# Reordering the gating front end of a convolution-and-attention kernel: a quarter of the moments on ScalarE, set-up products moved, parameter loads on another queue

## What is computed

```python
# L0: group norm, then a mixture of 4 experts, two of them for each pixel
g = gn(x)                                     # 32 groups of 3 channels, moments over 3*784 values
scores = softmax(tokens(g) @ gate_w + gate_b) # one row for each of 32*784 tokens, 4 experts
top_v, top_i = top_k(scores, 2); top_w = softmax(top_v)
present = one_hot(top_i).any(over tokens)     # which expert is first, which second anywhere
y_e = w2_e @ relu(w1_e @ g + b1_e) + b2_e     # 96 -> 96 -> 96 channels
coef_e = sum_k present[k, e] * top_w_k        # k = 0, 1
x = x + sum_e coef_e * y_e
# L1: attention over 8x8 heads (exp feature maps), then a feed-forward part with sign weights
t = t + attn(ln(t)) @ proj_w + proj_b
t = t + bitlinear(gelu(bitlinear(ln(t), W1, b1)), W2, b2)   # quantised in 5 groups of 6 images
```

## Time and profile before

| | us |
|---|---|
| median of 3 runs | 866.01 (865.44 to 871.82) |
| the profiled execution | 865.46, its span 863.7 |
| PE, DVE, ACT, POOL busy | 801.2, 642.9, 448.0, 190.0 |
| x landed (units 0 to 7) | about 50 |
| last gate product of unit 7 ends | 72.5 |
| first product for image 1 | 91.2 |

### The profile page before, as it was taken

One profiled execution on the slowest core, in us unless ns is written; L12 is line 12 of the kernel. 1 busy time (PEld: TensorE's weight loads), 2 busy tenths in 40 slices (PEclk: granted clock), 3 DMA queues, 4 the chain that ended last, 5 costly groups with the idle time before them and its releaser, 6 DMA issues.

```text
span 863.7 us, 17964 instructions
## 1 busy us (share of the span) xinstructions
PE 801.2 (93%) x6053; PEld 621.3 (72%) x6053; DVE 642.9 (74%) x1998; ACT 448.0 (52%) x619; POOL 190.0 (22%) x218
## 2 busy tenths in 40 slices
PE   1889799999999999999999999999999799999991
PEld 1456478888888888888888888888888655555550
DVE  3875377877777777777777777777677457988997
ACT  0232335445445445445445445445444299988981
POOL 2750022322222322322322322322322000000000
PEclk9999889999999999999999999999999899999996
DMA  9930001100001100000100000110010010473433
GB/s 216 230 88 1 15 15 36 52 29 28 28 28 29 54 28 28 28 28 28 56 28 28 28 28 28 54 30 28 28 42 14 15 43 0 145 192 102 149 112 112
DMA packets 19886, 48.54 MB, mean 56 GB/s; under 512 B 4558, under 2 KB 4754, under 8 KB 19858
## 3 DMA queue, kind: packets, MB, share of 16 engines
q1 hardware_dynamic: 17024, 46.97, 19.6%
q10 hardware_dynamic: 2834, 1.21, 0.8%
HBM read 29.51 MB, written 18.67 MB: 56 GB/s over the span
## 4 chain that ended last, share of the span: by engine, by line
PE 75%; DVE 9%; issue 6%; ACT 3%; POOL 3%; ACTq 2%; DVEq 1%; POOLq 0%
PE slot L960 17%; PE slot L941 12%; PE slot L820 10%; PE slot L1006 9%; PE slot L1127 5%; PE slot L1098 4%; PE slot L967 4%; PE slot L970 4%; PE slot L955 3%; DVE stage L1492 2%; ACTq L600 1%; DVE y2max L1499 1%; DVE xn L1518 1%; ACT hT L773 1%; PE slot L1159 1%
## 5 line engine op out<-in xcount | busy, mean ns | idle before, releaser
L960 PE MATMUL slot<-w2s,hT 128*112 128x96 f32 x1344 | 162.7, 269 | 0.0
L1375 DVE TENSOR_SCALAR xh<-t,ln_mv,ln_rs 112x96 f32<-112x96 f32 x434 | 109.2, 322 | 60.0 <-POOL ln_rs L577 60.0
L960 PEld LDWEIGHTS slot<-w2s,hT 128*112 128x112 f32 x1344 | 141.6, 177 | 10.8
L710 ACT ACTIVATE hT<-slot,b1c,w_unit 128x784 f32<-128x784 f32 x96 | 95.8, 1004 | 95.6 <-PE slot L941 95.6
L717 ACT ACTIVATE stage<-slot,minus_one 112x768 f32<-112x768 f32 x64 | 52.5, 820 | 118.0 <-PE slot L1006 118.0
L550 POOL TENSOR_TENSOR xn_lo<-xn,xn_hi 96x784 f16<-96x784 f32 x32 | 53.4, 1669 | 247.5 <-ACT xn_hi L699 247.3
L577 POOL TENSOR_TENSOR ln_rs<-ln_ve,pow_half 112x7 f32<-112x7 f32 x62 | 91.9, 1482 | 4.8
L967 PE MATMUL slot<-big,W1b 99*128 (+1 forms) x360 | 89.4, 329 | 0.6 <-ACT hT L773 0.6
L970 PE MATMUL slot<-big,W1b 96*128 (+1 forms) x360 | 89.2, 328 | 0.0
L1381 DVE TENSOR_REDUCE ymax<-slot 128x784 f32 (+1 forms) x90 | 83.8, 960 | 6.2 <-PE slot L970 5.9
L1006 PE MATMUL slot<-qkvw,xh1T 97*112 97x192 f32 x448 | 85.7, 333 | 0.9 <-ACT xh1T L729 0.9
(11 more groups left out here) (189 smaller groups left out, 1358.6 us busy)
## 6 DMA issues: line engine op xcount, KB each, us to landing
out<-t2T SPq DMA_DIRECT2D x56, 294.0 KB, 3.2
xs<-in_x SPq DMA_DIRECT2D x32, 294.0 KB, 3.1
big<-in_x SPq DMA_DIRECT2D x7, 1176.0 KB, 12.4
xs<-out SPq DMA_DIRECT2D x24, 294.0 KB, 3.3
big<-out SPq DMA_DIRECT2D x1, 1764.0 KB, 11.3
out<-big SPq DMA_DIRECT2D x6, 294.0 KB, 2.6
big<-in_x SPq DMA_DIRECT2D x2, 588.0 KB, 5.6
con<-shape_consts ACTq DMA_DIRECT2D x1, 445.5 KB, 6.1
```

The costliest lines, as they stand in the source:

```text
L710: nc.scalar.activation(hT[:, t, :].rearrange("p (a n) -> p a n", a=2), halves((0, one, 2)[t], P), ACT.Relu, scale=w1_unit[:, t:t + 1], bia ...
L960: ins = mm(o[:, j, :], hT[:, t, j * TOK:(j + 1) * TOK], w2s[:, v, t, :], start=False, stop=t == TILES - 1, skip_group_check=True)
L1375: ins = V.tensor_scalar(dst[:, j, :], src[:, j, :], ln_mv[n][:, j, 0:1], ln_rs[n][:, j:j + 1], ALU.subtract, ALU.mult)
```

## The change

- DVE leaves out one image in each unit from unit 1 on (image 3 of the unit, image 0 of the last one). ACT makes its moments (`statistics`): an Identity pass with an accumulator, a Square pass with an accumulator, a copy of one column. Each stands ahead of the `squares` of the same unit in ACT's list. `group_stats` waits for both engines.
- The 17 parameter loads go from ACT's queue to SP's, between the x of unit 1 and that of unit 2.
- POOL's three memsets of the ones rows go; one DMA on ACT's queue writes them from a small constant. Other POOL work is reordered around `gn_power`.
- PE: 26 `keep_busy` products ahead of unit 0; ahead of the `group_stats` of units 1 to 7 there are 2, 4, 4, 2, 2, 1 and 0 in place of 6. Unit 0 gets six behind. The transposes of the weights stand inside unit 4, the weight sums inside unit 6, between `group_between` and `gate_unit`. `logit_tokens(0)` stands ahead of unit 7 and writes another PSUM slot.
- DVE: the w1 scale and small memsets ahead of unit 3, the weight reductions behind unit 5, the weight means and the lambda chain between units 6 and 7. `first_weights_in(0)` and `first_shares(0)` stand ahead of `pairs_compared(3)`, `first_weights(0)` ahead of the flags, `first_weights_in(1)` between the two reads of image 0's mix.
- ACT: `norm_first`, `squares`, `logit_rows` and the exponentials in the order that this needs.

```diff
+        gn_nm = sb("gn_nm", [C, UNITS])
+        two_ones = sb("two_ones", [PARTS, HALF])
+        spare = stage[0:C, 5376:5376 + HALF].bitcast(F16)
...
+        CONSTS_SET = (ones_ready, 10)
...
+        def act_image(u):
+            return 0 if u == UNITS - 1 else UNIT - 1
...
@@ -423,6 +432,23 @@
             for r in range(2):
                 sp.dma_start(x_all[:, 4 * r:4 * r + 4, :],
...
+            def load(dst, src):
+                sp.dma_start(dst, src).then_inc(params_loaded, 16)
+
+            load(w1_raw[:, :, :], w1.rearrange("e d c -> (e d) c").rearrange("(t p) c -> p t c", p=P))
...
+            load(W1_raw[:, :, :], W1.rearrange("(t p) c -> p t c", p=P))
...
+            load(fb2c[:, :], fb2.rearrange("(c a) -> c a", a=1))
             for u in range(2, UNITS - 1):
                 sp.wait_ge(x_loaded[u % 2], 16 * (u // 2))
                 sp.dma_start(x_all[:, u * UNIT:(u + 1) * UNIT, :],
...
-            for u in range(3):
-                gn_power(u)
-                nc.gpsimd.memset(big[C:C + PARTS, u * QIMAGES // 3:(u + 1) * QIMAGES // 3, 0, :].bitcast(F32),
-                                 TWO_ONES).then_inc(bigones_ready, 1)
+            gn_power(0)
+            gn_power(1)
             xn_rest(0, 0)
+            gn_power(2)
+            xn_rest(1, 1)
+            pool.wait_ge(params_loaded, 16 * N_PARAMS)
             gn_power(3)
-            pool.wait_ge(params_loaded, 16 * N_PARAMS)
             rows = slice(C, C + PARTS)
             bf16_parts(fb1r[rows, :], rows, HID, con[rows, K_PART96:K_PART96 + 2])
             gn_power(4)
             bf16_rest(W1b[rows, :], rows, HID, con[rows, K_PART96:K_PART96 + 2])
-            xn_rest(1, 1)
...
             bf16_parts(b2r[:, :], rows, C, con[rows, K_PART:K_PART + 2])
+            gn_power(6)
             bf16_rest(b2_parts[:, :], rows, C, con[rows, K_PART:K_PART + 2])
-            gn_power(6)
             gn_power(7)
...
-            def load(dst, src):
-                act.dma_start(dst, src).then_inc(params_loaded, 16)
...
-            load(w1_raw[:, :, :], w1.rearrange("e d c -> (e d) c").rearrange("(t p) c -> p t c", p=P))
...
-            load(fb2c[:, :], fb2.rearrange("(c a) -> c a", a=1))
             act.wait_ge(*CONSTS_SET)
             act.dma_start(projb[0:1, :], proj_b.rearrange("(a n) -> a n", a=1)).then_inc(projb_loaded, 16)
+            act.dma_start(big[C:C + PARTS, 0:QIMAGES, 0, :].bitcast(F32),
...
+            def statistics(u):
+                act.wait_ge(x_loaded[u % 2], 16 * (u // 2 + 1))
+                j = act_image(u)
+                image = x_all[:, u * UNIT + j, :]
+                wait_count(act, act_moment, 2 * (u - 1))
+                nc.scalar.activation(spare, image, ACT.Identity, scale=-1.0 / (HW * np.sqrt(HW)),
+                                     accum_out=gn_nm[:, u:u + 1]).then_inc(act_moment, 1)
+                wait_count(act, gn_group, u - 1)
+                act.wait_ge(act_moment, 2 * u - 1)
+                nc.scalar.activation(spare, image, ACT.Square, scale=1.0 / np.sqrt(HW), bias=gn_nm[:, u:u + 1],
+                                     accum_out=gn_mv[:, u % 2, j, 1:2]).then_inc(act_moment, 1)
+                nc.scalar.activation(gn_mv[:, u % 2, j, 0:1], gn_nm[:, u:u + 1], ACT.Copy,
+                                     scale=-float(np.sqrt(HW))).then_inc(act_mv_ready, 1)
...
             squares(0)
+            statistics(1)
+            norm_first(0)
             squares(1)
+            norm_first(1)
+            statistics(2)
             logit_rows(0)
             squares(2)
-            norm_first(0)
-            squares(3)
-            logit_rows(1)
+            statistics(3)
             act.wait_ge(params_loaded, 16 * N_PARAMS)
...
             ins.then_inc(w1_scaled, 1)
-            norm_first(1)
+            squares(3)
+            statistics(4)
+            logit_rows(1)
+            squares(4)
+            statistics(5)
             act.wait_ge(setup_T, 1)
-            nc.scalar.activation(lam_e[:, 0:2], S[2][0:C, 0, 400:402], ACT.Exp)
...
                 setup_copied, 1)
-            squares(4)
             squares(5)
+            statistics(6)
             logit_rows(2)
+            squares(6)
+            statistics(7)
             act.wait_ge(wmean_ready, 1)
             for g in range(QGROUPS):
...
-            squares(6)
+            squares(7)
+            gate_exps(0, 0)
...
             ins.then_inc(signs_ready, 1)
+            logit_rows(3)
...
                         relu(t, n)
+                        if n == 0:
+                            gate_exps(0, 1)
...
-                    gate_exps(0, 0)
                     act.wait_ge(signs_ready, 1)
                     nc.scalar.copy(W2last[:, :], W2b[:, TILES - 1, :])
-                    gate_exps(0, 1)
...
-            squares(7)
-            logit_rows(3)
...
             def group_stats(u):
                 pe.wait_ge(gn_mv_ready, u + 1)
+                wait_count(pe, act_mv_ready, u)
...
-                        ins = tr(S[3][0:TOK, g, o:o + rows], lrow[2 * g + b][0:rows, c * TOK:(c + 1) * TOK],
+                        ins = tr(S[2 + g][0:TOK, g, o:o + rows], lrow[2 * g + b][0:rows, c * TOK:(c + 1) * TOK],
...
+            def setup_transposed():
+                pe.wait_ge(params_loaded, 16 * N_PARAMS)
+                pe.wait_ge(w1_scaled, 1)
+                for t in range(TILES):
+                    tr(S[2][0:C, 0, t * P:(t + 1) * P], w1_raw[:, t, :])
...
+                pe.wait_ge(lam_prod, 1)
+                mm(S[2][0:C, 0, 400:402], con[0:C, K_HEAD:K_HEAD + C], lam_e[:, 2:4],
+                   start=True, stop=True, skip_group_check=True).then_inc(setup_T, 1)
...
+            def weight_sums():
+                pe.wait_ge(wsum_ready, 1)
+                mm(S[3][0:C, 0, 400:400 + QGROUPS], ones_f[0:C, 0:C], wsum[0:C, 0, :], start=True, stop=True,
...
+            def unit(u, ahead, inside=None, behind=6):
                 if u >= 3 and u % 2 == 1:
                     ranks(u // 2 - 1)
                 if u >= 1:
                     wait_count(pe, gn_nmean_ready, u - 1)
-                    if u % 2 == 1:
-                        wait_count(pe, lbias_ready, u // 2)
-                    keep_busy(0, u % 2, 6)
+                    if ahead:
+                        if u % 2 == 1:
+                            wait_count(pe, lbias_ready, u // 2)
+                        keep_busy(0, u % 2, ahead)
                 group_stats(u)
                 if u >= 2 and u % 2 == 0:
                     pair_differences(u // 2 - 1)
                 group_between(u)
-                if u >= 1:
-                    pe.wait_ge(gn_nmean_ready, u)
-                    if u % 2 == 0:
-                        pe.wait_ge(lbias_ready, u // 2)
-                    keep_busy(0, (u + 1) % 2, 6)
+                if inside is not None:
+                    inside()
+                wait_count(pe, gn_nmean_ready, u)
+                if u >= 2 and u % 2 == 0:
+                    pe.wait_ge(lbias_ready, u // 2)
+                keep_busy(0, (u + 1) % 2, behind)
                 gate_unit(u)
 
+            pe.wait_ge(*CONSTS_SET)
+            keep_busy(0, 1, 26)
             pe.wait_ge(gate_params, 16 * N_GATE_PARAMS)
-            pe.wait_ge(*CONSTS_SET)
-            unit(0)
-            unit(1)
-            unit(2)
-            unit(3)
-            pe.wait_ge(params_loaded, 16 * N_PARAMS)
-            pe.wait_ge(w1_scaled, 1)
-            for t in range(TILES):
...
-            unit(4)
...
-            unit(5)
-            unit(6)
-            unit(7)
+            unit(0, 0)
+            unit(1, 2)
+            unit(2, 4)
+            unit(3, 4)
+            unit(4, 2, setup_transposed, 1)
+            unit(5, 2)
+            unit(6, 1, weight_sums, 5)
+            pe.wait_ge(setup_copied, 2)
+            logit_tokens(0)
+            unit(7, 0)
...
                     pair_differences(GATES - 1)
-                    pe.wait_ge(setup_copied, 2)
+                    pe.wait_ge(gate_exp_in, 1)
                     hidden(2, 2, r)
                     ranks(GATES - 1)
-                    pe.wait_ge(signs_ready, 1)
-                    for g in range(2):
-                        logit_tokens(g)
+                    logit_tokens(1)
...
                 for j in range(UNIT):
+                    if u > 0 and j == act_image(u):
+                        continue
                     if j == UNIT // 2 and between is not None:
                         between(u // 2 - (2 if between is ranks_seen else 1))
...
                 for j in range(UNIT):
+                    if u > 0 and j == act_image(u):
+                        continue
                     ins = V.bn_aggr(gn_mv[:, u % 2, j, :], gn_st[:, u % 2, j, :, :].rearrange("p h k -> p (h k)"))
...
             bn_unit(1)
             V.tensor_copy(rank_w[:, :], con[0:PAIR_ROWS, K_RANK:K_RANK + SIDE])
             bn_unit(2)
-            bn_unit(3, pairs_compared)
```

(27 more changed lines are left out.)

64 lines of the change are left out of this document (31 added, 33 removed).

## The result

The changed kernel took 856.23 us (median of 4 runs, 854.21 to 859.98), beside 868.91 for the kernel before on the same chip. The ratio is 0.988 [0.9852, 0.9908], some 8 to 13 us faster, where 850, 16 us less than before, had been forecast. The profiled execution took 857.24, with a span of 855.4. Against the profiled execution of before (865.46, span 863.7) the span is 8.3 us shorter, where 15.85 had been summed. Executions of one and the same code differ by several us here, because the stretches at a granted clock of 0.50 fall in other places and are of other lengths; so the places in the front end and the loop are compared in the traces, and the totals with their intervals. The ratios are taken from fast runs alone and are not the quotients of the medians; one slow run further down, of 862.26 us, is in its kernel's median and not in its ratio.

The account below looks back on a forecast made before the run. PE's start of image 1 was taken as bound by engines lagging the loads, then DVE's hand-over. Gains 9.5 + 0.45 + 3.6 + 2.3 = 15.85 us took 865.46 to 849.6, median 850.2, stated as 850; range 844 to 857.

Parts of the forecast that it names:

- Part 1: Front end: moments on two engines and fewer `keep_busy` bring unit 7's group products to 57.0 from 67.99, 11.0 us earlier.
- the walk: Last three units with x landing as before: moments ready at 44.5, 50.0 and 56.9 us, DVE needing 3.8 or 4.1 each.
- Part 2: Front-end loads: parameters on SP's queue cost x 0.9 us and the ones rows 0.6, so x comes up to 1.5 later.
- it does not run dry: SP's load queue stays filled by parameters, since SP reaches unit 2 at about the time unit 1 lands.
- Part 3 and 4: Hand-over to image 1: fewer transposes between hidden tiles gain 0.45 us; PE's gap falls from 4.24 to 0.65, gaining 3.6.
- Part 5: Image 1's start: without a long gap 18 products take 3.0 us; third relu after 3.25 instead of 5.58, gaining 2.3.
- The slow stretch at 114: In the image loop: the half-clock stretch at 114.3 us might shift away, gaining 2.0 us beyond the forecast.
- the better rival: x not delayed (1.5 us), slow stretch at 114.3 shifted away (2.0): 848.5 or 848 by one, 846.5 by both; chance 0.12.
- The clock in unit 7: PE's wait before unit 7's group products lowers the clock, costing 2.4 us or twice 4.8: 852.5 to 855; chance 0.17.

Follow-up runs that it names:

- same code again: The changed kernel run and profiled once more with no edit: 855.52 us, ratio 0.9884 to the kernel before.

## Why the prediction was right or wrong

The profile of after gained 8.30 us where 15.85 had been summed. Of the 7.55 missing, 3.87 lie behind the loop, 2.52 ahead of the group products of unit 7 and 1.23 in unit 7; the 1.69 lost in the loop are made up by 1.72 that had not been counted on.

- **Part 1, the walk: right, once x is on time.** Three images cost DVE 3.8 or 4.1 a unit, as summed, and the last moments come at 58.1 with x at 40.66 (forecast 56.9). Two things that bring it are worth up to 3 us each: ACT's quarter (the kernel with all moments on DVE; 1.8 to 3.3, of which the loop takes 1.6 back) and the fewer `keep_busy` (six again; 0.5 to 3.3). DVE's new wait for the weight sums was 2.5 to 3.2 where about 2.0 had been taken; `ranks_seen`, POOL and ACT cost nothing more, as said. Taking that wait away brought the group products of unit 7 no earlier (61.05), because DVE then waits for PE's differences and PE's own list ends no sooner.
- **Part 2, the loads: the step that failed.** The ones rows were costed by their bytes at x's rate, 0.6 us; they cost 3.3 (44.39 against 41.07). The parameters' order was costed at 0.9 and is worth 0.4 to 1.0. That "it does not run dry" held only with the ones rows out of the way. Together 3.7 against 1.5, so 2.2 of the missing 2.5 us up to the group products of unit 7; the longer wait for the weight sums is the rest. With both taken away the group products came 2.8 us earlier (58.18), not 3.7, as the wait for the weight sums grew to 3.22. The row that should have warned is one of bytes and engines at once: the DMA took 6.0% of 16 engines for 12 us, 11.5 us of one engine. Spread over 16 that is 0.7, over three 3.8. The second is near what was measured, in this kernel as in that with the parameters on ACT (6.6% of 11 us, again 11.6, and x 3.5 late). The destination has three rows, and beside x never more than three of the DMA's packets are under way at once, in both orders (behind x, up to six). But the trace does not show on which engines a transfer lies, and no run changed the number of rows, so this is argued and not shown; shown is that this DMA, beside x, costs 3.3 us, and behind x nothing that can be told. (The Trainium skill, "DMA: Bandwidth & Descriptors", section "Why a DMA increments its semaphore by 16 and not by 1", says that a copy from SP or ACT is split over the largest number of engines up to 16 that divides the slowest dimension of both sides, which would be three here. The trace agrees in size.)
- **Part 3 and 4, logits and gap: right.** 3.99 against 0.45 + 3.6 = 4.05, in 13 of the 14 profiles with the new hand-over (the other is that of the ones rows late, with its 10.2 us at 0.50), and 0.01 in the one without.
- **Part 5, clock of image 1: right.** At the third relu of image 1, the place of the forecast's 2.3, it is 2.40 in all three profiles of the table with the new hand-over, and 0.09 in the one without. That the whole way from image 1 to the end of the loop also gives 2.43 in the profile of after is luck: it is 2.40 + 1.72 - 1.69.
- **The slow stretch at 114: half of the better rival took place.** Its 2.0 us shared a chance of 0.12 with x on time. In the profile of after they came, as 1.72; in same code again, with 3.4 us at 0.50 from 116.1 on, 0.12 of them.
- **The loop: a term put at nothing that is 1.7 us.** The prediction took the loop to cost the same, because its code is the same. It is 1.69 us longer in each of the 14 profiles of kernels with ACT's moments, and 0.05 in the one without. What in ACT's moments does it stays open.
- **The clock in unit 7: the rival with 0.17 took place.** After has 3.4 us at 0.50 from 62.3 on, and the way from the group products to the hidden product is 6.16 instead of 4.93: 1.2 us, of which the stretch makes 1.0, since the profiles without `keep_busy` and without a stretch have 5.15 to 5.18. Such a stretch came in 9 of the 12 profiles that run no `keep_busy` ahead of unit 7, between 58.9 and 65.6, and lasted 3.4 in all but one. The price lay below what the rival had (2.4 to 4.8), but in that one, with 10.2 us, it was 4.2; the chance lay above. What PE did before it fits the rival: it was idle for 1.0 to 2.1 us ahead of the group products in 11 profiles of changed kernels, and 9 of these have the stretch; it was not idle in 4, and none has it. Filling that idle time brought no total down.
- **What no part had: the later clock.** The prediction took the feed-forward part to cost the same too. At the end of the loop after is 12.17 us ahead, at the end of the span 8.3. PE runs 20.5 us at 0.50 at the passage, where before has 6.8 and the same code again 3.4. The way from the first relu of image 30 to the end goes with it in the changed kernels: 222.7 to 223.7 us with 3.4 us in the one stretch there, 223.8 to 224.4 with 6.8, 229.1 in all five with 20.5 (225.1 before). It is not a loss that the change always brings, but the sum was made against one execution, and between executions this term moves by several us, more than most of the terms that had been worked out. Its cause, and why some kernels show it more often, stays open.

The version with the ones rows late and the parameters on ACT is the one to keep: 848.92 and 850.34 (849.38 without the run of 862.26), ratios 0.9796 [0.9736, 0.9855] and 0.9781 [0.9736, 0.9825]. Of the 5 to 8 us between it and the change the trace shows 3 to 4 as place at image 1; the rest goes with the clock (mean granted clock 0.981 to 0.985 in seven of its ten runs, 0.971 to 0.981 in the eight of the changed kernel), and is not explained.

## What to carry over

Cost a DMA that runs beside a load on the path by the engine time of its packets and by how few engines may have to carry it, not by its bytes alone, and put one that is needed late behind the loads. When a wait goes, ask which instruction of the same engine waits next: the wait for the weight sums was 2.5 us and worth nothing. Code that a change leaves alone need not keep its pace: measure one turn of the loop before and after. And before working out terms below 3 us, see how far two executions of one code differ in the stretches at the lower clock; where they differ by as much, compare landmarks in the traces and not the totals.

## What the runs showed of the hardware

- A pass of ACT with an accumulator is two instructions: 0.86 or 0.95 us for 96 x 784, and 0.19 for reading the sum.
- A DMA of 0.14 MB into three rows held back loads of x by 3.3 us. SP was held as well: three small loads took 7.31 us to issue beside it (6.8 to 7.4 in six profiles), 4.30 in the one without.
- Stretches at 0.50 lasted 3.4, 6.8, 10.2, 13.7 or 20.5 us, apart from the one at the span's end. Products that filled PE's idle time ahead of unit 7 left no stretch there, in three profiles of three, but each has one of 6.8 us later (at 83, 82 and 101 us). At the passage the places of the stretches in one code (666 and 679 us) lie as far apart as those with and without the products (673), so nothing is shown of the products there.
- In a loop whose code is the same, DVE began one operation 0.23 us behind the PE products it waits for, in every second image, where it was 0.11, as long as ACT's moments were in the kernel's front end. The cause is not shown.
